# Moving a 128-point Hadamard transform from the FFN's activations onto its down weights, in a two-block transformer tower on one core

## Chip, cores, metric

The kernel is one program on one core of a Trainium2 chip. The metric is device time in microseconds (us). The engines are TensorE (PE in the profile; its weight loads are listed apart as PEld), VectorE (DVE), ScalarE (ACT), GpSimd (POOL) and SyncE (SP), which here issues all the transfers. Each engine runs its own instructions in program order and waits on semaphores for the others.

## The reference, cut to what matters

256 tokens of width 512 (64 sequences of 4 positions) pass a patch embedding, a first attention with quantised activations and ternary weights, a mixture of 16 experts with top-2 routing, a second attention, and an FFN with Hadamard transforms. Only the last is touched:

```python
n = SU_ug.shape[0]                       # 512
x = fwht(x * SU_ug) / SCALE
x_up = x @ W_up.T * (Wscale_ug[:INTER] * SCALE)
x_gate = x @ W_gate.T * (Wscale_ug[INTER:] * SCALE)
x = jax.nn.silu(x_gate) * x_up           # 256 tokens x 2048
x = fwht(x * SU_dp) / SCALE              # 2048-point transform
x = x @ W_down.T * (Wscale_dp * SCALE)   # 2048 -> 512
```

`fwht` is the normalised Walsh-Hadamard transform, a symmetric matrix of +1 and -1. The 2048 features lie as 16 chunks of 128: partitions hold the position in a chunk. The 2048-point transform is therefore a 128-point transform inside each chunk and a 16-point one across the chunks. Since both are linear, either can be applied to the activations or to the rows of the down weights.

## The kernel before, in words

Products are made in a split form: each fp32 operand is a high part (rounded by ACT to fp32r) plus a low part (the rest, taken by DVE), and three products high-high, high-low and low-high are added in PSUM. Names with `_hi` and `_lo` are these parts. A few products, the transposes (line 668) and the sums over prod (lines 787 and 939), are plain fp32.

The order on each engine is written out by hand. In the order of time:

- First attention (to about 64 us of the profiled span). At its end PE makes `transposes(2)`, issues 20 filler matmuls (`keep_warm`, line 701, products nobody reads), then `transposes(3)`; the router and the experts follow.
- Experts, `unit(n)` and `dn(p)`. Beside them DVE folds `down_raw` (the down weights, 16 chunks of 128x512) with the part of the 16-point transform that combines chunks c, c+4, c+8, c+12: `fold_piece(0)` to `fold_piece(3)` for the chunks 0, 1, 4, 5, 8, 9, 12, 13, then pieces 4 to 7 for the others. When all is done DVE sets `fold_done`.
- Second attention (from about 180 us). PE: `warm_up(2, ...)` with 24 fillers, `transposes(4)`, 5 fillers, the qkv products of token tile 0 and 1, then for each tile t fillers (3 and 8), `values(t)` and the output projection.
- FFN, `for f in range(FC)`. `ffn_gu(f)` on PE makes gate and up of chunk f, 24 matmuls of 256 columns. ACT takes the silu, DVE the product (`fglu`, line 1619, into `M["h"]`), ACT the high part of it (`fh_hi`, line 648), DVE the low part (`fh_ready`, line 1624), and PE the 128-point transform of chunk f, `rotate(f)`: two matmuls (lines 1000 and 1001) into bank 3 or 7. After four chunks ACT copies one bank to `M["a"]` (line 655) and DVE adds and subtracts (`within_pairs`, lines 1590 and 1591; `across_pairs`, line 1600), which is the rest of the 16-point transform. Then u is split (`u_high`, `u_low`) and multiplied by the split down weights (`wd_high`, `wd_low`, `down(c)`, 6 matmuls of 512 columns), which run some 7 chunks behind.
- SP issues the loads in one order. `l1_w` (second attention's weights, 2560 KB) stands before a wait for `side_done` 8, and `down_w` (4096 KB) behind the wait, since it overwrites the weights of the first attention. `f_low(f)` (line 1493) is the low part of the FFN weights of chunk f.

`tb(t, n)` is PSUM bank 4t + n. The functions that the change touches:

Of the kernel before, what the change touches and what calls it, by code (L numbers as in the profile page):

```python
# [75 lines left out]
def tower(nc, patches, tok_w, tok_b, att_w, router, moe_gu, moe_dn, l1_w, vec_cols, ws_dp, ffn_w,  # L76
          down_w, consts, out):
    with ExitStack() as ctx:
# [94 lines left out]
        fsilu, fglu, fh_hi, fh_ready = sem("fsilu"), sem("fglu"), sem("fh_hi"), sem("fh_ready")  # L173
        hd_done, hd_copied, hd_read = sem("hd_done"), sem("hd_copied"), sem("hd_read")
# [5 lines left out]
        XT_BANK = (1, 2, 1, 2, 1)  # L180

# [60 lines left out]
        with ExitStack() as s:  # L242
            M["silu"] = [sb(f"fs{j}", [P, TOK], F32, s) for j in range(2)]
            M["h"] = [sb(f"fh{j}", [P, TOK], F32, s) for j in range(2)]
            M["h_hi"] = [sb(f"fhh{j}", [P, TOK], F32R, s) for j in range(4)]
            M["h_lo"] = [sb(f"fhl{j}", [P, TOK], F32R, s) for j in range(4)]
            M["a"] = sb("fa", [P, 2, TOK], F32, s)
# [98 lines left out]
        def _(sp):  # L346
# [22 lines left out]
            sp.dma_start(l1_raw[:], l1_w).then_inc(ld_l1, 16)  # L369
            sp.wait_ge(side_done, 8)  # L370
            sp.dma_start(big_raw[:], down_w).then_inc(ld_down, 16)
            for p in range(2, PAIRS):
# [58 lines left out]
        def _(act):  # L431
# [100 lines left out]

            xt_high(2)
            xt_high(3)
            act.wait_ge(h_ready0, 2)
# [46 lines left out]

            xt_high(4)
            xt_high(5)
# [37 lines left out]
            def wd_high(c):  # L622
                if c == 0:
                    act.wait_ge(fold_done, 1)
                if c >= 4:
                    act.wait_ge(down_done, c - 3)
# [9 lines left out]
            for f in range(FC):  # L636
# [26 lines left out]
        def _(pe):  # L663
# [145 lines left out]

            transposes(2, B["xn"], 0)  # L810
            keep_warm(bank[3], GAP)
# [82 lines left out]
            for n in range(3):  # L894
                unit(n, False)
# [20 lines left out]
            warm_up(2, bank[3], WARM[1])  # L916
            transposes(4, L["xn"], 0)
            keep_warm(bank[3], 5)
            pe.wait_ge(w1_ready, KC)
            for t in range(TILES):  # L920
                for dst, a, b in ((tb(t, 3)[:, 0:QKV1 - C], C, QKV1), (tb(t, 2)[:], 0, C)):
                    pe.wait_ge(xt_hi_ready, 5 + t)
# [20 lines left out]
            for t in range(TILES):  # L943
                warm_up(3 + t, bank[1], 3 + 5 * t)
# [7 lines left out]

            transposes(8, M["xn"], 0)
# [40 lines left out]
            def rotate(f):  # L994

                pe.wait_ge(fh_ready, f + 1)
                if f >= 4 and f % 4 < 2:
                    pe.wait_ge(hd_read if f % 2 else hd_copied, f // 4)
                dst = tb(f % 2, 3)[:, f % 4 // 2 * TOK:(f % 4 // 2 + 1) * TOK]
# [713 lines left out]
```

## Time and profile before

| what | value |
|---|---|
| median of 3 runs | 301.54 us (300.75 to 302.03) |
| profiled execution, its own time | 300.32 us |
| its span, first to last instruction | 298.5 us |
| busy: PE / DVE / ACT | 275.4 (92%) / 236.9 (79%) / 146.8 us (49%) |
| mean granted TensorE clock | 0.973 |

The span is 1.8 us shorter than the time of the same execution. Busy shares are means over stages that are limited by different engines, so they tell little alone. PE's busy time includes the filler matmuls, which are 122 in number.

### The profile page before, as it was taken

How to read it: one execution, taken by the hardware profiler on the slowest of the kernel's cores; microseconds unless marked ns; L12 is line 12 of the kernel's file. 1: busy time of each engine (PE TensorE's matmuls, PEld its weight loads, DVE VectorE, ACT ScalarE, POOL GpSimd, SP SyncE). 2: the span in 40 equal slices, each digit the busy share in tenths (PEclk: the TensorE clock that was granted, in tenths of full speed). 3: DMA queues.
4: the chain of work that ended last, by engine and by line, in shares of the span. 5: the costliest groups of instructions: out<-in, count | busy, mean ns of one | idle time of the engine just before them, and what ended most of it. 6: DMA issues, size and time to landing. Idle time of an engine off the chain costs nothing. (4 is left out here: it accounts for less than half of the span.)

```text
span 298.5 us, 4692 instructions
## 1 busy us (share of the span) xinstructions
PE 275.4 (92%) x1807; PEld 238.3 (80%) x1807; DVE 236.9 (79%) x439; ACT 146.8 (49%) x238; POOL 10.0 (3%) x30
## 2 busy tenths in 40 slices
PE   8899399599989999999999999977999999999993
PEld 3555266499979899999999979857899999999862
DVE  1979997878496999899898877798628895778683
ACT  3989640024644665645655432322137773773640
POOL 0200000010000000000000004000000000000000
PEclk9999789977999999999999999999999999999998
DMA  6941599905034835546400049094000000000003
GB/s 255 414 186 36 187 378 418 419 4 189 26 137 183 307 117 211 193 157 242 151 0 3 0 143 419 2 356 209 0 0 2 0 3 0 2 1 2 0 0 70
DMA packets 6567, 40.47 MB, mean 136 GB/s; under 512 B 1169, under 2 KB 1425, under 8 KB 5266
## 3 DMA queue, kind: packets, MB, share of 16 engines
q1 hardware_dynamic: 6546, 40.18, 35.4%
q8 instruction: 14, 0.23, 0.3%
q14 instruction: 7, 0.06, 0.1%
HBM read 39.13 MB, written 0.52 MB: 133 GB/s over the span
## 5 line engine op out<-in xcount | busy, mean ns | idle before, releaser
L870 PE MATMUL bank<-s_xt_hi,s_gu_hi 128*128 128x256 f32 x120 | 34.0, 283 | 0.0
L871 PE MATMUL bank<-s_xt_lo,s_gu_hi 128*128 128x256 f32 x120 | 33.9, 283 | 0.0
L872 PE MATMUL bank<-s_xt_hi,s_gu_lo 128*128 128x256 f32 x120 | 33.9, 282 | 0.0
L984 PE MATMUL bank<-s_xf_hi,s_f_hi 128*128 128x256 f32 x128 | 31.3, 283 | 0.1
L984 PE MATMUL bank<-s_xf_hi,s_f_lo 128*128 128x256 f32 x128 | 31.1, 282 | 0.0
L459 ACT CAST s_xt_hi<-bank 128x512 fp32r<-128x512 f32 x10 | 5.9, 587 | 39.2 <-PE bank L668 33.3
L984 PEld LDWEIGHTS bank<-s_xf_hi,s_f_hi 128*128 128x128 f32 x128 | 24.1, 188 | 0.7 <-ACT s_xf_hi L619 0.4
L1493 DVE TENSOR_TENSOR s_f_lo<-s_ffn_raw,s_f_hi 128x1024 fp32r<-128x1024 f32 x16 | 19.6, 1225 | 6.1 <-ACT s_f_hi L592 6.1
L984 PEld LDWEIGHTS bank<-s_xf_hi,s_f_lo 128*128 128x128 f32 x128 | 24.1, 188 | 0.3
L871 PEld LDWEIGHTS bank<-s_xt_lo,s_gu_hi 128*128 128x128 f32 x120 | 23.0, 191 | 0.2
L870 PEld LDWEIGHTS bank<-s_xt_hi,s_gu_hi 128*128 128x128 f32 x120 | 23.0, 191 | 0.3
L872 PEld LDWEIGHTS bank<-s_xt_hi,s_gu_lo 128*128 128x128 f32 x120 | 23.0, 191 | 0.0
L466 ACT CAST s_gu_hi<-s_moe_raw 128x1024 fp32r<-128x1024 f32 x16 | 16.7, 1047 | 10.4 <-PE bank L872 10.3
L674 PE MATMUL bank<-s_dn_hi,s_ht_hi 128*128 128x512 f32 x48 | 19.3, 401 | 1.9 <-DVE s_ht_lo L1370 1.4
L526 ACT CAST s_ht_hi<-s_hm 128x256 fp32r<-128x256 f32 x24 | 9.6, 407 | 22.0 <-DVE s_hm L1364 22.0
L1288 DVE TENSOR_TENSOR s_gu_lo<-s_moe_raw,s_gu_hi 128x1024 fp32r<-128x1024 f32 x16 | 19.4, 1217 | 0.5 <-ACT s_gu_hi L466 0.5
L701 PE MATMUL bank<-s_had 128*128 128x256 f32 x122 | 18.9, 307 | 0.6 <-DVEq L1538 0.6
L639 ACT ACTIVATE s_fs<-bank,s_cols 128x256 f32<-128x256 f32 x16 | 7.6, 475 | 23.1 <-PE bank L990 23.1
L676 PE MATMUL bank<-s_dn_hi,s_ht_lo 128*128 128x512 f32 x48 | 18.8, 391 | 0.0
L675 PE MATMUL bank<-s_dn_lo,s_ht_hi 128*128 128x512 f32 x48 | 18.8, 391 | 0.0
L701 PEld LDWEIGHTS bank<-s_had 128*128 128x128 f32 x122 | 17.0, 207 | 1.6 <-DVEq L1538 1.0
L872 PE MATMUL bank<-s_xt_hi,s_rest_lo 128*128 128x256 f32 x64 | 18.1, 283 | 0.0
(249 smaller groups left out, 725.0 us busy)
## 6 DMA issues: line engine op xcount, KB each, us to landing
s_moe_raw<-moe_gu SPq DMA_DIRECT2D x16, 768.0 KB, 5.9
s_ffn_raw<-ffn_w SPq DMA_DIRECT2D x4, 2048.0 KB, 9.8
s_moe_raw<-moe_dn SPq DMA_DIRECT2D x8, 768.0 KB, 4.3
s_big_raw<-att_w SPq DMA_DIRECT2D x4, 1024.0 KB, 8.0
s_big_raw<-down_w SPq DMA_DIRECT2D x1, 4096.0 KB, 25.3
s_l_raw<-l_w SPq DMA_DIRECT2D x1, 2560.0 KB, 15.2
out<-s_h SPq DMA_DIRECT2D x4, 128.0 KB, 2.3
s_tok_w<-tok_w SPq DMA_DIRECT2D x1, 256.0 KB, 2.7
```

Of the source, the lines that this page charges most:

```text
L466: act.copy(B["gu_hi"][e % 2][:], main_of(e)).then_inc(guh_ready, 1)
L526: act.copy(B["ht_hi"][p % 2][:, part, :], B["hm"][n % 4][:]).then_inc(h_hi, 1)
L674: pe.matmul(dst, x_hi, w_hi, start=first, stop=False)
L675: pe.matmul(dst, x_hi, w_lo, start=False, stop=False)
L676: return pe.matmul(dst, x_lo, w_hi, start=False, stop=last)
L701: pe.matmul(spare_bank[:, 0:TOK].rearrange("p (i n) -> p i n", i=2), had[:], had[:].unsqueeze(1).to_broadcast([P, 2, P]), start=True, stop ...
L870: pe.matmul(dst, w_hi, xt_hi[:, k, :], start=(k == 0), stop=False)
L871: pe.matmul(dst, w_hi, xt_lo[:, k, :], start=False, stop=False)
L872: last = pe.matmul(dst, w_lo, xt_hi[:, k, :], start=False, stop=(k == KC - 1))
L984: pe.matmul(tb(j, n)[:, 0:TOK], M[w][j][:, k, n * P:(n + 1) * P], M["xf_hi"][:, k, :], start=(w == "w_hi" and k == 0), stop=False)
L1288: dve.tensor_tensor(B["gu_lo"][e % 2][:], main_of(e), B["gu_hi"][e % 2][:].bitcast(F32), ALU.subtract).then_inc(gu_ready, 1)
L1493: dve.tensor_tensor(M["w_lo"][f % 2][:], ffn_chunk_raw(f), M["w_hi"][f % 2][:].bitcast(F32), ALU.subtract).then_inc(fw_ready, 1)
```

## The change

The 128-point transform is applied to each chunk of `down_raw` instead of each chunk of h. `turn(i)` on PE makes one plain fp32 product of the Hadamard matrix (in `con`) with a chunk of 128x512 and `turned_back(i)` on ACT copies the bank back over the chunk. Eight chunks (those that `fold_piece(0)` to `(3)` combine) are turned before the fold, at the end of the first attention; the other eight after it, in the second attention. They stand where fillers stood. `down_w` is loaded ahead of `l1_w`. In the FFN `rotate`, the split of h and the copy to `M["a"]` are gone; `within_pairs` reads h itself from SBUF.

```diff
+        TURN_FIRST, TURN_LAST = (0, 1, 4, 5, 8, 9, 12, 13), (2, 3, 6, 7, 10, 11, 14, 15)
 (SP)
-            sp.dma_start(l1_raw[:], l1_w).then_inc(ld_l1, 16)
             sp.wait_ge(side_done, 8)
             sp.dma_start(big_raw[:], down_w).then_inc(ld_down, 16)
+            sp.dma_start(l1_raw[:], l1_w).then_inc(ld_l1, 16)
 (ACT)
+            def turned_back(i, ps):
+                c = (TURN_FIRST + TURN_LAST)[i]
+                act.wait_ge(turn_done, i + 1)
+                act.copy(down_raw[:, c, :], ps[:]).then_inc(turned, 1)
...
+            for i in range(3):
+                turned_back(i, bank[3 + 4 * (i % 2)])
             xt_high(2)
+            for i in range(3, 7):
+                turned_back(i, bank[3 + 4 * (i % 2)])
             xt_high(3)
+            turned_back(7, bank[7])
...
+            for i in range(8, 11):
+                turned_back(i, bank[3 + 4 * (i % 2)])
             xt_high(4)
+            turned_back(11, bank[7])
             xt_high(5)
...
             f_high(1)
+            turned_back(12, bank[1])
             xt_high(6)
             exp(3, L["sc"][:, 2, 1, 0:4], L["sc"][:, 3, 1, 0:4])
+            turned_back(13, bank[5])
             act.activation(spare1[:], neg_half[:], ACT.Silu)
+            turned_back(14, bank[1])
+            turned_back(15, bank[5])
             xt_high(7)
...
-                act.wait_ge(fglu, f + 1)
-                if f >= 4:
-                    act.wait_ge(hd_done, f - 3)
-                act.copy(M["h_hi"][f % 4][:], M["h"][j][:]).then_inc(fh_hi, 1)
                 for c in wd_of(f):
                     wd_high(c)
-                if f % 4 == 3:
-                    act.wait_ge(hd_done, f)
-                    if f >= 4:
-                        act.wait_ge(hd_read, f // 4)
-                    act.copy(M["a"][:], tb(0, 3)[:].rearrange("p (i n) -> p i n", i=2)).then_inc(hd_copied, 1)
 (PE)
+            def turn(i, ps, copied):
+                c = (TURN_FIRST + TURN_LAST)[i]
+                if i == 0:
+                    pe.wait_ge(ld_down, 16)
+                if i == len(TURN_FIRST):
+                    pe.wait_ge(fold_done, 1)
+                if copied:
+                    pe.wait_ge(turned, copied)
+                pe.matmul(ps[:], con[:, K_H:K_H + P], down_raw[:, c, :], start=True, stop=True).then_inc(turn_done, 1)
...
+            for i in range(3):
+                turn(i, bank[3 + 4 * (i % 2)], max(i - 1, 0))
             transposes(2, B["xn"], 0)
-            keep_warm(bank[3], GAP)
+            for i in range(3, 8):
+                turn(i, bank[3 + 4 * (i % 2)], i - 1)
             transposes(3, B["xn"], 1)
...
-            warm_up(2, bank[3], WARM[1])
+            for i in range(8, 11):
+                turn(i, bank[3 + 4 * (i % 2)], i - 1 if i > 9 else i)
             transposes(4, L["xn"], 0)
-            keep_warm(bank[3], 5)
+            turn(11, bank[7], 10)
             pe.wait_ge(w1_ready, KC)
+            pe.wait_ge(turned, 11)
...
-                warm_up(3 + t, bank[1], 3 + 5 * t)
+                if t == 0:
+                    turn(12, bank[1], 12)
+                else:
+                    turn(13, bank[5], 12)
+                    turn(14, bank[1], 13)
+                    turn(15, bank[5], 14)
                 values(t)
...
-            def rotate(f):
-                pe.wait_ge(fh_ready, f + 1)
...
-                pe.matmul(dst, had[:], M["h_hi"][f % 4][:], start=True, stop=False)
-                pe.matmul(dst, had[:], M["h_lo"][f % 4][:], start=False, stop=True).then_inc(hd_done, 1)
...
-                if f >= 1:
-                    rotate(f - 1)
 (DVE)
-                    dve.wait_ge(ld_down, 16)
+                    dve.wait_ge(turned, len(TURN_FIRST))
...
-                dve.wait_ge(hd_copied, g + 1)
-                dve.wait_ge(hd_done, 4 * g + 4)
-                odd = tb(1, 3)[:].rearrange("p (i n) -> p i n", i=2)
-                o.mark(dve.tensor_tensor(half_rotated[:, 0:2], M["a"][:], odd, ALU.add))
+                dve.wait_ge(fglu, 4 * g + 4)
+                even, odd = M["h"][g % 2][:, 0:4:2, :], M["h"][g % 2][:, 1:4:2, :]
+                o.mark(dve.tensor_tensor(half_rotated[:, 0:2], even, odd, ALU.add))
...
-                dve.wait_ge(fh_hi, f + 1)
-                dve.tensor_tensor(M["h_lo"][f % 4][:], M["h"][j][:], M["h_hi"][f % 4][:].bitcast(F32), ALU.subtract
-                                  ).then_inc(fh_ready, 1)
```

PE at the end of the first attention before, from its last projection products to the transposes of the second token tile (`s_con` holds both the identity and the Hadamard matrix, `s_had` is the filler's operand):

```order
L795 MATMUL bank4<-s_tern_p,s_xt_hi 128x512 x4
L687 MATMUL bank4<-s_tern_p,s_xt_lo 128x512 x4
L668 MATMUL bank2<-s_con,s_prod0 128x128 x4
L701 MATMUL bank3<-s_had 128x256 x20
L668 MATMUL bank6<-s_con,s_prod0 128x128 x4
```

The same place now; `s_big_raw` is the down weights:

```order
L695 MATMUL bank4<-s_tern_p,s_xt_lo 128x512 x4
L727 MATMUL bank3<-s_big_raw,s_con 128x512
L727 MATMUL bank7<-s_big_raw,s_con 128x512
L727 MATMUL bank3<-s_big_raw,s_con 128x512
L676 MATMUL bank2<-s_con,s_prod0 128x128 x4
L727 MATMUL bank7<-s_big_raw,s_con 128x512
L727 MATMUL bank3<-s_big_raw,s_con 128x512
L727 MATMUL bank7<-s_big_raw,s_con 128x512
L727 MATMUL bank3<-s_big_raw,s_con 128x512
L727 MATMUL bank7<-s_big_raw,s_con 128x512
L676 MATMUL bank6<-s_con,s_prod0 128x128 x4
```

Three fp32 products stand ahead of the first transposes, where nothing stood, and five take the place of the 20 fillers.

PE at the start of the second attention before, from the last expert product to the first qkv products:

```order
L676 MATMUL bank4<-s_dn_hi,s_ht_lo1 128x512
L701 MATMUL bank3<-s_had 128x256 x24
L668 MATMUL bank1<-s_con,s_xn2 128x128 x4
L701 MATMUL bank3<-s_had 128x256 x5
L681 MATMUL bank3<-s_w1_hi,s_xt_hi 128x256
```

The same place now:

```order
L684 MATMUL bank4<-s_dn_hi,s_ht_lo1 128x512
L727 MATMUL bank3<-s_big_raw,s_con 128x512
L727 MATMUL bank7<-s_big_raw,s_con 128x512
L727 MATMUL bank3<-s_big_raw,s_con 128x512
L676 MATMUL bank1<-s_con,s_xn2 128x128 x4
L727 MATMUL bank7<-s_big_raw,s_con 128x512
L689 MATMUL bank3<-s_w1_hi,s_xt_hi 128x256
```

Three products replace 24 fillers ahead of the transposes, and one replaces 5 behind them.

DVE at the end of the FFN before, from the product of the last chunk on (`s_fh` is h, `s_fhl` its low part, `s_fa` is `M["a"]`):

```order
L1619 SCALAR_TENSOR_TENSOR s_fh1<-bank5,s_cols,s_fs1 128x256
L1624 TENSOR_TENSOR s_fhl3<-s_fh1,s_fhh3 128x256
L1611 TENSOR_TENSOR s_wd_lo<-s_big_raw,s_wd_hi 128x512
L1590 TENSOR_TENSOR s_half_rotated<-s_fa,bank7 128x512
L1591 TENSOR_TENSOR s_half_rotated<-s_fa,bank7 128x512
```

The same place now:

```order
L1642 SCALAR_TENSOR_TENSOR s_fh1<-bank5,s_cols,s_fs1 128x256
L1632 TENSOR_TENSOR s_wd_lo<-s_big_raw,s_wd_hi 128x512
L1611 TENSOR_TENSOR s_half_rotated<-s_fh1 128x512
L1612 TENSOR_TENSOR s_half_rotated<-s_fh1 128x512
L1632 TENSOR_TENSOR s_wd_lo<-s_big_raw,s_wd_hi 128x512
```

The low part of h is gone, and the additions of pairs follow the product with one other operation between.

## Rows read from the trace of the kernel before

**Rows 1.** Windows: PE, PEld, DVE, ACT, POOL busy, clock, DMA share, GB/s

```profile
65.00:179.70 114.70, 112.75 (x792) 105.67 (x792) 99.89 (x173) 61.03 (x111) 0.00 (x0) 0.99 0.37 136
179.70:219.40 39.70, 35.68 (x240) 31.81 (x239) 28.52 (x56) 9.87 (x17) 5.17 (x12) 1.00 0.44 179
219.40:287.00 67.60, 67.27 (x490) 63.00 (x488) 52.56 (x84) 41.30 (x73) 0.00 (x0) 1.00 0.01 1
```

**Rows 2.** Timeline around the end of the FFN: start, us, engine, line [idle before]

```profile
280.67 0.28 PE L1000 MATMUL bank<-s_fhh,s_had 128*128 128x256 f32 x1
280.79 0.28 PE L1001 MATMUL bank<-s_fhl,s_had 128*128 128x256 f32 x1
...
280.94 0.48 DVE L1619 SCALAR_TENSOR_TENSOR s_fh<-bank,s_cols,s_fs 128x256 f32<-128x256 f32 x1 [0.94 <-ACT s_fs L639]
...
282.42 0.69 DVE L1611 TENSOR_TENSOR s_wd_lo<-s_big_raw,s_wd_hi 128x512 fp32r<-128x512 f32 x1
...
283.03 0.68 DVE L1590 TENSOR_TENSOR s_half_rotated<-s_fa,bank 128x512 f32<-128x512 f32 x1
...
287.46 0.47 PE L674 MATMUL bank<-s_wd_hi,s_u_hi 128*128 128x512 f32 x1 [0.36 <-DVE s_u_lo L1606]
```

**Rows 3.** Instructions of line 787: duration in ns, first and last start

```profile
L787 PE MATMUL bank<-s_prod,s_con x16: 590/593/593, 42.2 to 48.6; 128*128 128x512 f32 x16
```

**Rows 4.** Windows of PE alone: busy, clock, DMA share, GB/s

```profile
42.20:49.00 6.80, 6.80 (x18) 1.00 0.98 368
...
61.00:64.00 3.00, 2.66 (x13) 0.50 0.00 0
...
68.00:70.50 2.50, 2.50 (x13) 0.50 0.00 0
```

**Rows 5.** Timeline of SP's issues before the experts' loads

```profile
35.81 0.48 SPq L369 DMA_DIRECT2D s_l_raw<-l_w  x1
36.33 0.44 SPq L371 DMA_DIRECT2D s_big_raw<-down_w  x1
```

**Rows 6.** The page's DMA issues: count, KB each, median us to landing

```profile
s_big_raw<-down_w SPq DMA_DIRECT2D x1, 4096.0 KB, 25.3
s_l_raw<-l_w SPq DMA_DIRECT2D x1, 2560.0 KB, 15.2
```

**Rows 7.** Timeline of PE at the end of the first attention

```profile
55.21 1.07 PE L687 MATMUL bank<-s_tern_p,s_xt_lo 128*128 128x512 f32 x4
59.40 0.66 PE L668 MATMUL bank<-s_con,s_prod 128*128 128x128 f32 x4 [3.12 <-DVE s_prod L1048]
59.81 3.85 PE L701 MATMUL bank<-s_had 128*128 128x256 f32 x20
64.09 0.68 PE L668 MATMUL bank<-s_con,s_prod 128*128 128x128 f32 x4 [0.43 <-DVE s_prod L1048]
```

**Rows 8.** Timeline at the start of the second attention

```profile
179.72 3.04 PE L701 MATMUL bank<-s_had 128*128 128x256 f32 x24
...
182.59 0.60 PE L668 MATMUL bank<-s_con,s_xn 128*128 128x128 f32 x4
...
183.23 0.59 ACT L459 CAST s_xt_hi<-bank 128x512 fp32r<-128x512 f32 x1 [4.02 <-PE bank L668]
...
183.96 0.36 PE L681 MATMUL bank<-s_w_hi,s_xt_hi 128*128 128x256 f32 x1 [0.17 <-ACT s_xt_hi L459]
...
189.65 0.69 DVE L1517 TENSOR_TENSOR s_prod<-s_kv,s_q 128x512 f32<-128x512 f32 x1 [0.90 <-ACT s_q L600]
```

**Rows 9.** Timeline of PE around the two value sums

```profile
194.84 2.02 PE L939 MATMUL bank<-s_con,s_prod 128*128 128x128 f32 x16 [0.54 <-DVE s_prod L1551]
...
199.81 0.86 PE L687 MATMUL bank<-s_o_hi,s_xt_lo 128*128 128x512 f32 x3
...
203.37 3.81 PE L939 MATMUL bank<-s_con,s_prod 128*128 128x128 f32 x32 [0.93 <-DVE s_prod L1551]
```

**Rows 10.** The page's costly groups: line, count, busy us, mean ns, idle before

```profile
L1493 DVE TENSOR_TENSOR s_f_lo<-s_ffn_raw,s_f_hi 128x1024 fp32r<-128x1024 f32 x16 | 19.6, 1225 | 6.1 <-ACT s_f_hi L592 6.1
```

More of the change, by code:

```diff
@@ L172, in tower @@
         fwh_ready, fw_ready, fg_done, fu_done = sem("fwh_ready"), sem("fw_ready"), sem("fg_done"), sem("fu_done")
-        fsilu, fglu, fh_hi, fh_ready = sem("fsilu"), sem("fglu"), sem("fh_hi"), sem("fh_ready")
-        hd_done, hd_copied, hd_read = sem("hd_done"), sem("hd_copied"), sem("hd_read")
+        fsilu, fglu = sem("fsilu"), sem("fglu")
+        turn_done, turned, hd_read = sem("turn_done"), sem("turned"), sem("hd_read")
         u_raw, u_hi, u_ready, wdh_ready, wd_ready, down_done = sem("u_raw"), sem("u_hi"), sem("u_ready"), sem("wdh_ready"), sem("wd_ready"), sem("down_done")
@@ L243, in tower @@
             M["silu"] = [sb(f"fs{j}", [P, TOK], F32, s) for j in range(2)]
[L244 to L247, printed above, removed]
+            M["h"] = [sb(f"fh{j}", [P, 4, TOK], F32, s) for j in range(2)]
             M["u"] = sb("u", [P, 4, TOK], F32, s)
@@ L624, in wd_high @@
                     act.wait_ge(fold_done, 1)
+                    act.wait_ge(turned, FC)
                 if c >= 4:
@@ L894, in _ @@
             for n in range(3):
+                if n == 2:
+                    pe.wait_ge(turned, 8)
                 unit(n, False)
@@ L913, in _ @@
             dn(PAIRS - 1)
-            warm_up(2, bank[3], WARM[1])
+            for i in range(8, 11):
+                turn(i, bank[3 + 4 * (i % 2)], i - 1 if i > 9 else i)
             transposes(4, L["xn"], 0)
-            keep_warm(bank[3], 5)
+            turn(11, bank[7], 10)
             pe.wait_ge(w1_ready, KC)
+            pe.wait_ge(turned, 11)
             for t in range(TILES):
                 for dst, a, b in ((tb(t, 3)[:, 0:QKV1 - C], C, QKV1), (tb(t, 2)[:], 0, C)):
+                    if t == 1:
+                        pe.wait_ge(turned, 12)
                     pe.wait_ge(xt_hi_ready, 5 + t)
@@ L950, in _ @@
                 low_products(tb(t, 3)[:], t, lambda k: L["o_hi"][:, k, :]).then_inc(proj_done, 1)
+            pe.wait_ge(turned, FC)
             transposes(8, M["xn"], 0)
@@ L992, in ffn_gu @@
                     last.then_inc(done, 1)
-            def rotate(f):
-                pe.wait_ge(fh_ready, f + 1)
-                if f >= 4 and f % 4 < 2:
-                    pe.wait_ge(hd_read if f % 2 else hd_copied, f // 4)
-                dst = tb(f % 2, 3)[:, f % 4 // 2 * TOK:(f % 4 // 2 + 1) * TOK]
-                pe.matmul(dst, had[:], M["h_hi"][f % 4][:], start=True, stop=False)
-                pe.matmul(dst, had[:], M["h_lo"][f % 4][:], start=False, stop=True).then_inc(hd_done, 1)
             def down_tile(c, t):
@@ L1016, in _ @@
                 ffn_gu(f)
-                if f >= 1:
-                    rotate(f - 1)
                 if f >= 7:
                     down(f - 7)
-            rotate(FC - 1)
             for c in range(9, FC - 4):
@@ L1585, in within_pairs @@
             def within_pairs(g):
-                dve.wait_ge(hd_copied, g + 1)
-                dve.wait_ge(hd_done, 4 * g + 4)
-                odd = tb(1, 3)[:].rearrange("p (i n) -> p i n", i=2)
-                o.mark(dve.tensor_tensor(half_rotated[:, 0:2], M["a"][:], odd, ALU.add))
-                dve.tensor_tensor(half_rotated[:, 2:4], M["a"][:], odd, ALU.subtract).then_inc(hd_read, 1)
+                dve.wait_ge(fglu, 4 * g + 4)
+                even, odd = M["h"][g % 2][:, 0:4:2, :], M["h"][g % 2][:, 1:4:2, :]
+                o.mark(dve.tensor_tensor(half_rotated[:, 0:2], even, odd, ALU.add))
+                dve.tensor_tensor(half_rotated[:, 2:4], even, odd, ALU.subtract).then_inc(hd_read, 1)
             def across_pairs(g):
@@ L1618, in _ @@
                 dve.wait_ge(fu_done, f + 1)
-                dve.scalar_tensor_tensor(M["h"][j][:], tb(j, 1)[:, 0:TOK], wsu_c[:, f:f + 1], M["silu"][j][:],
+                if f >= 8:
+                    dve.wait_ge(hd_read, f // 4 - 1)
+                dve.scalar_tensor_tensor(M["h"][f // 4 % 2][:, f % 4, :], tb(j, 1)[:, 0:TOK], wsu_c[:, f:f + 1], M["silu"][j][:],
                                          ALU.mult, ALU.mult).then_inc(fglu, 1)
```

## The prediction, as put on record before the kernel ran

> **What bounds the kernel now.** I read the windows by stage first, to see which engine is full where. PE is busy 112.75 of 114.70 us in the experts and 67.27 of 67.60 us in the FFN, while DVE has 99.89 and 52.56 us of work there and ACT 61.03 and 41.30; in the second attention PE has 35.68 of 39.70 us, and part of that is fillers [rows 1]. So real PE work that leaves the FFN shortens it one for one, and PE time added in place of fillers costs only what overhangs them. Then the timelines of the places that the change touches, to see who waits for whom. At the end of the first attention PE sits idle 3.12 us and then runs 20 fillers; both transposes wait for DVE's xn (the releaser in both rows) [rows 7]. At the start of the second attention the chain is xn, transposes, ACT's copy, qkv products, and DVE waits 0.90 us for q at 189.65 [rows 8]: what delays PE there delays all that follows. At the very end PE waits 0.36 us for DVE's u_low [rows 2]: the last stretch hangs on DVE's chain from the last h.
>
> **What leaves the FFN.** `rotate` is two matmuls per chunk, issued 0.12 us apart (280.67, 280.79) although each lasts 0.28, since they overlap [rows 2]. A chunk costs PE 2 x 0.12 = 0.24 us. Fifteen rotates stand ahead of the last chunk's gate and up: 15 x 0.24 = 3.6 us, all on the full engine. From then on the end is set by DVE. Before, 2.09 us pass from the last h (280.94) to the first addition of pairs (283.03), filled by ACT's high part, DVE's low part, the last rotate, ACT's copy and one wd_low [rows 2]. Now only h (0.48) and wd_low stand there. Lengths include an overlap with the next instruction, so I take 0.48 + 0.69 = 1.17, plus 0.1 for ACT's cast of wd, which wd_low waits for: 1.26. Gain 0.83. Behind the first addition DVE's queue is the same as before, back to back up to u_low. PE arrives there 16 x 0.24 = 3.84 earlier for its matmuls and some 0.4 earlier for the last rotate that held it, against 4.43 for DVE, so its wait of 0.36 stays about as it is. **FFN: -(3.6 + 0.83) = -4.4 us.** The additions read h from SBUF instead of one operand from a bank; I take the same 0.68 us. ACT's 16 casts and 4 copies and DVE's 16 low parts are worth nothing by themselves, PE being the full engine.
>
> **What a turn costs.** The trace has no such product, but line 787 has the same shape in fp32 with moving data of 512 columns. Its loop issues 8 products and the trace shows 16 instructions, so one is two. Their starts run from 42.2 to 48.6: 6.4/15 = 0.43 us apart, 0.86 per product, the last ending 0.59 after its start [rows 3], at a granted clock of 1.00 [rows 4]. ACT's copy of a bank is 0.59 us [rows 8]. A release takes 0.04 us from PE to ACT (182.59 + 0.60 = 183.19 to 183.23) and 0.14 from ACT to PE (183.82 to 183.96) [rows 8].
>
> **First attention.** Before, PE's last product ends at 56.28 and the next could be issued at some 56.12. Three turns end their issue at 56.12 + 3 x 0.86 = 58.70, under the idle time to 59.40 with 0.7 us to spare [rows 7]. The weights must be there: before, `down_w` lands at 36.33 + 25.3 = 61.6 and `l1_w` at 35.81 + 15.2 = 51.0 [rows 5, 6]. The two land one behind the other, 10.6 us for 4096 KB, so 2560 KB take 6.6 us and `down_w` ahead of them lands at 55.0, 1.1 us before PE asks. `l1_w` then lands near 61.6, where `down_w` did, and is first read by ACT in the experts. Five turns follow the transposes at 59.81. Two banks alternate, so two turns take at least product 1.02, release 0.04, copy 0.59, release 0.14 = 1.79, 0.90 a turn; with the first at 0.86 they end at 64.10 to 64.25 against 64.09 for the transposes [rows 7]. ACT's copy for the router stands behind turned copy 6, which is done by then. **+0.15 us**, and PE's fullness in the experts [rows 1] passes it on. The DVE fold waits for 8 turned chunks only some 30 us later, at no cost.
>
> **Second attention, start.** Turn 8 begins at 179.72 where the 24 fillers did and ends at 180.74. Turn 9 waits for its copy: 180.78 + 0.59 + 0.14 = 181.51. Turn 10 follows at 182.37 and the transposes at 183.22, against 182.59. ACT takes copy 9 before, then copy 10 from 183.42 to 184.01, and only then the copy of xt, which waits in ACT's queue behind it: to 184.60, PE at 184.74 against 183.96 [rows 8]. Turn 11 (183.62 to 184.48) is under that. The whole stage follows q: **+0.75 us**.
>
> **Second attention, values.** Turn 12 takes the place of 3 fillers and 0.54 us of idle before 194.84 and fits. Turns 13 to 15 can be issued when the projection's products are out, at 199.81 + 3 x 0.23 = 200.51, without the fillers' wait for DVE. They need 3 x 0.86 to 203.1, or 203.2 since turn 15 waits for copy 13, which stands behind ACT's exp; the value sum began at 203.37 after 0.93 us of idle [rows 9]. From there PE runs 3.81 us by itself, so an overhang would cost in full. I take **+0.05 us**. Their copies finish well before ACT's next xt.
>
> **Sum.** -4.4 + 0.15 + 0.75 + 0.05 = -3.5 us. The profiled execution took 300.32 us, which gives 296.8. It lies 1.2 us under the median of the runs, 301.54, from which I count: **298.0 us**. A measurement of this kernel can tell about 0.5%, 1.5 us, from no change.
>
> **The rivals.**
>
> *The clock falls under the turns.* Before, the clock was 0.50 at 61 to 64, after the idle at 56 to 59, and 0.50 at 68 to 70.5, after the router's products of 16 columns [rows 4, 7]. A turn at the lower level (1.2 instead of 2.4 GHz) takes 1.71 us. If turns 3 to 7 run there, 5 x 0.86 = +4.3, which gives 302.3. Against it: three turns now lie in that idle time, and fp32 products back to back kept 1.00 for 6.8 us [rows 4]. Chance 0.08. The Trainium skill (TensorE: Matmul & The Clock Gate, "A second HAM failure mode: psum-queue depth-cycling") says that a stream which cycles through PSUM banks, with small waits between its groups, can make the clock swing, which is the pattern of turn, copy, turn. The trace so far speaks against it; by the page this rival would be the forecast.
>
> *The weights come late (slower).* If `down_w` does not land ahead of `l1_w` but with it, near 61.6, turn 0 starts 5.5 us late, less 0.7 to spare: +4.8, so 302.8; an idle time of that length lowers the clock as the shorter one did, and turns 0 to 7 at 1.71 add up to 6.9: 302.8 to 309.7, say 305. It decides from a landing at 56.1 + 0.7 + 3.5 = 60.3 on. Against it stand the two landings 10.6 us apart. Chance 0.05. The Trainium skill (DMA: Bandwidth & Descriptors, "Queues, rings and completion order") has descriptors of one ring consumed in order but no first-in-first-out completion for an issuing engine; here the share of the DMA engines was 0.98 while the two loads ran [rows 4], each load being spread over all of them, so I keep it small.
>
> *DVE or ACT becomes the FFN's bound.* Without `rotate` a chunk is 24 x 0.12 = 2.88 us of PE. In chunks 4 to 6 DVE has h 0.48, f_low 1.23 [rows 2, 10] and two operations of 0.68: 3.1 at most. If the first six rotates are not given back, 6 x 0.24 = 1.4 us is lost: 299.4. For it speaks that DVE's margin is thin there; against it that before the ratio was the same (DVE 0.4 more, PE 0.24 more) and PE had no gap. Chance 0.10.
>
> *More than that.* The denser stream could keep the clock up through 68 to 70.5 too; the 3 us at half rate would give 1.5 back: 296.5. The router's small products stay as they are. Chance 0.08.
>
> **The numbers.** The forecast, 297 to 299.3, has 0.69. With the rivals at 302.3, 305, 299.4 and 296.5 the range 295.8 to 300.6 leaves out the first two and a little on each side, under 0.2; its upper end takes in an overhang of some 1 us in each attention beside a smaller gain at the end. Faster by over 0.5% (under 300.0): 0.69 + 0.10 + 0.08 less some at the edges = 0.84. Within: 0.10, of which most is the clock's rival. Slower: 0.06.
>
> **What would show it.** The turn's group: 32 instructions of 0.59, 0.43 apart; `down_w` landing at 55 with PE's idle time before turn 0 gone; transposes at 64.2, qkv products 0.9 later than before, the value sums not later than that; in the FFN a chunk shorter by 0.24 with PE at 99%; from the last h to the first addition some 1.25 us. It is wrong if turns are spaced by more than 0.9, if the clock under them shows 0.50, or if PE in the FFN gets idle before DVE.

## The result, and the profile after

| | before | changed |
|---|---|---|
| median of 6 interleaved runs | 301.86 us | 298.31 us |
| lowest to highest | 300.75 to 303.58 | 294.98 to 298.71 |
| profiled execution | 300.32 us | 297.94 us |
| its span, mean granted clock | 298.5 us, 0.973 | 296.1 us, 0.979 |

The changed kernel takes 0.987 of the time before (95% interval 0.9831 to 0.9909): 3.55 us less by the medians, where 3.5 was forecast. A second set of runs of it gave 297.59 us, 0.9864 (0.9823 to 0.9905).

The two profiled spans differ by 2.4 us only, because the one after starts late: the last group of PE's products in the first attention (four, shown as one row) begins at 56.57 us, against 55.21 before [rows 7]. This event is the reference event in all that follows. The delay is there before anything that was changed: the first transfer of the swapped keys goes out at 28.45 us, against 26.92 before, since ACT waited 0.5 us longer for the first attention weights and 1.0 us longer for DVE. A second profiled execution of the changed kernel has that transfer at 27.25. So a good part of the delay is chance; that all of it is, is not shown, for the reference event lies at 55.2 to 56.0 in the three profiles with the old order of loads and at 55.9 to 57.6 in the nine with the new one. Everything below is therefore measured from an event that both kernels have, not from the start of the span.

**The weights.** The timeline of SP's issues after, and the page's DMA issues (count, KB each, us to landing):

```profile
37.84 0.33 SPq L368 DMA_DIRECT2D s_big_raw<-down_w  x1
38.22 0.45 SPq L369 DMA_DIRECT2D s_l_raw<-l_w  x1
```
```profile
s_big_raw<-down_w SPq DMA_DIRECT2D x1, 4096.0 KB, 20.0
s_l_raw<-l_w SPq DMA_DIRECT2D x1, 2560.0 KB, 25.6
```

`down_w` lands at 37.84 + 20.0 = 57.84 and the other at 63.8, one behind the other again, as before [rows 5, 6]. With the late start added, the forecast of 55.0 becomes 56.4: it is 1.4 us late, and all of the 1.1 us to spare is used up. The 20.0 us are this execution's; in the eight other profiles with this order the load took 18.3 or 18.4 us. The later landing of `l1_w` (63.8 instead of 51.0) cost nothing, as the length of the experts below shows.

**The turns.** All instructions of the turned products: duration in ns (least, median, most), first and last start, shapes:

```profile
L727 PE MATMUL bank<-s_big_raw,s_con x32: 590/592/697, 57.9 to 205.0; 128*128 128x512 f32 x32
```

The timeline of PE at the end of the first attention of the changed kernel (start, us, engine, line, operation, count, [idle before <-releaser]):

```profile
56.57 1.07 PE L695 MATMUL bank<-s_tern_p,s_xt_lo 128*128 128x512 f32 x4
57.89 2.93 PE L727 MATMUL bank<-s_big_raw,s_con 128*128 128x512 f32 x6 [0.24 <-DMA s_big_raw<-down_w]
60.76 0.66 PE L676 MATMUL bank<-s_con,s_prod 128*128 128x128 f32 x4
61.25 4.63 PE L727 MATMUL bank<-s_big_raw,s_con 128*128 128x512 f32 x10
65.72 0.60 PE L676 MATMUL bank<-s_con,s_prod 128*128 128x128 f32 x4
```

Turn 0 waits 0.24 us for the weights. Three turns (6 instructions) still fit under what was 3.12 us of idle time: the transposes come 60.76 - 56.57 = 4.19 us after the reference event, and before it was 59.40 - 55.21 = 4.19 [rows 7]. The five turns behind them take 4.47 us to the second transposes; in all 9.15 us pass, against 8.88 before, so this place costs +0.27, where +0.15 was forecast. Windows of the same kernel (PE, PEld, DVE, ACT, POOL busy, clock, DMA share, GB/s) show the clock under the turns at full:

```profile
52.00:68.00 16.00, 15.66 (x72) 9.68 (x70) 12.93 (x29) 6.94 (x12) 1.61 (x4) 1.00 0.55 235
69.00:72.00 3.00, 3.00 (x16) 3.00 (x16) 2.67 (x8) 0.35 (x2) 0.00 (x0) 0.50 0.00 0
```

The stretch at half clock behind the router is there as it was before [rows 4]. From the second transposes to PE's first instruction behind the last expert product it is 115.57 us, and was 115.63.

**Second attention, start**, PE and ACT in the timeline of the changed kernel:

```profile
181.29 1.02 PE L727 MATMUL bank<-s_big_raw,s_con 128*128 128x512 f32 x2
182.35 0.59 ACT L464 COPY s_big_raw<-bank 128x512 f32<-128x512 f32 x1 [1.55 <-PE bank L727]
182.99 1.98 PE L727 MATMUL bank<-s_big_raw,s_con 128*128 128x512 f32 x4 [0.68 <-ACT s_big_raw L464]
184.81 0.60 PE L676 MATMUL bank<-s_con,s_xn 128*128 128x128 f32 x4
185.01 0.59 ACT L464 COPY s_big_raw<-bank 128x512 f32<-128x512 f32 x1 [0.27 <-PE bank L727]
185.49 0.59 ACT L457 CAST s_xt_hi<-bank 128x512 fp32r<-128x512 f32 x1
186.23 0.36 PE L689 MATMUL bank<-s_w_hi,s_xt_hi 128*128 128x256 f32 x1
```

It went as worked out: turn 9 waits 0.68 us for copy 8, and ACT takes copy 10 ahead of the cast of xt. The first product of the projection comes 186.23 - 181.29 = 4.94 us after the first turn, against 183.96 - 179.72 = 4.24 after the first filler [rows 8]: +0.70, forecast +0.75.

**Values**, PE in the timeline of the changed kernel:

```profile
201.82 1.09 PE L695 MATMUL bank<-s_o_hi,s_xt_lo 128*128 128x512 f32 x4
202.75 2.82 PE L727 MATMUL bank<-s_big_raw,s_con 128*128 128x512 f32 x6
205.62 3.81 PE L967 MATMUL bank<-s_con,s_prod 128*128 128x128 f32 x32
```

The last value sum starts 2.25 us later than before [rows 9], and the first projection product of this attention came 186.23 - 183.96 = 2.27 later. Turns 12 to 15 cost nothing.

**FFN.** Stages of the changed kernel as windows (columns as above), and the timeline of DVE at its end:

```profile
67.00:181.30 114.30, 112.35 (x788) 105.23 (x789) 99.88 (x173) 61.18 (x111) 0.00 (x0) 0.99 0.38 137
181.30:221.60 40.30, 37.70 (x216) 29.43 (x214) 28.43 (x56) 14.05 (x25) 5.17 (x12) 1.00 0.43 175
221.60:284.00 62.40, 61.95 (x455) 58.58 (x455) 46.77 (x67) 33.67 (x52) 0.00 (x0) 1.00 0.00 1
```
```profile
279.56 0.48 DVE L1642 SCALAR_TENSOR_TENSOR s_fh<-bank,s_cols,s_fs 128x256 f32<-128x256 f32 x1 [1.84 <-ACT s_fs L656]
280.05 0.69 DVE L1632 TENSOR_TENSOR s_wd_lo<-s_big_raw,s_wd_hi 128x512 fp32r<-128x512 f32 x1
280.66 0.69 DVE L1611 TENSOR_TENSOR s_half_rotated<-s_fh 128x512 f32<-128x512 f32 x1
```
```profile
286.22 0.51 PE L682 MATMUL bank<-s_wd_hi,s_u_hi 128*128 128x512 f32 x1 [0.18 <-DVE s_wd_lo L1632]
```

PE stays full (61.95 of 62.40 us), and the gap between it and the others has grown: DVE has 46.77. Counted from PE's first product of the transform that opens the stage (215.53 before, 217.79 after), the last h comes 3.64 us earlier than before (forecast 3.6). From the last h to the first addition of pairs it is 280.66 - 279.56 = 1.10 us where it was 2.09 [rows 2] (forecast 1.26). With both, the FFN is 4.61 us shorter to DVE's last addition, that of the residual (78.99 before, 74.38 after).

The sum of the profiled spans: +1.36 before any changed instruction, +0.27, -0.06 in the experts, +0.70, 0 and -4.61 make -2.34, and 298.5 - 296.1 is 2.4. Without the late start it is -3.7, beside -3.55 by the medians of the runs.

### The profile page after: what moved, and what is told of

Read it like the earlier page. It is cut to its first block and busy times, and to the rows that moved or that the text cites. A ratio compares the mean times of both kernels' runs of the same rounds, so it can differ in the third digit from the quotient of the medians.

```text
span 296.1 us, 4530 instructions
## 1 busy us (share of the span) xinstructions
PE 276.2 (93%) x1744; PEld 231.0 (78%) x1747; DVE 231.7 (78%) x423; ACT 148.7 (50%) x234; POOL 10.0 (3%) x30
## 5 line engine op out<-in xcount | busy, mean ns | idle before, releaser
L893 PE MATMUL bank<-s_xt_lo,s_rest_hi 128*128 128x256 f32 x64 | 18.1, 283 | 0.0
L892 PE MATMUL bank<-s_xt_hi,s_rest_hi 128*128 128x256 f32 x64 | 18.1, 283 | 0.0
L1024 PE MATMUL bank<-s_xf_lo,s_f_hi 128*128 128x256 f32 x128 | 17.8, 281 | 0.0
```

The costliest lines, as they stand in the source:

```text
L892: pe.matmul(dst, w_hi, xt_hi[:, k, :], start=(k == 0), stop=False)
L893: pe.matmul(dst, w_hi, xt_lo[:, k, :], start=False, stop=False)
L1024: last = pe.matmul(tb(j, n)[:, 0:TOK], M["w_hi"][j][:, k, n * P:(n + 1) * P], M["xf_lo"][:, k, :], start=False, stop=(k == KC - 1))
```

## The experiments

The kernel before ran beside each; a ratio is to it. Theory: the gain is all in the FFN (PE's rotates and the shorter chain), the turns are almost free since they stand in place of idle time and fillers, and they are free only because `down_w` lands first. The rivals: the turns change the clock; the FFN is bound by DVE, so that its casts and low parts are what paid.

**One half alone.** `e1_ffn_only` is the kernel before with the edits to the FFN's h and `rotate` only, so the 128-point transform is left out. `e2_turns_only` has the turns and the order of loads and keeps `rotate`.

```
 e1 (to before):
-                act.copy(M["h_hi"][f % 4][:], M["h"][j][:]).then_inc(fh_hi, 1)
...
-                if f >= 1:
-                    rotate(f - 1)
 e2 (to before):
-            sp.dma_start(l1_raw[:], l1_w).then_inc(ld_l1, 16)
             sp.wait_ge(side_done, 8)
             sp.dma_start(big_raw[:], down_w).then_inc(ld_down, 16)
+            sp.dma_start(l1_raw[:], l1_w).then_inc(ld_l1, 16)
...
+            for i in range(8, 11):
+                turn(i, bank[3 + 4 * (i % 2)], i - 1 if i > 9 else i)
```

> The kernel before with only the FFN half of the change: rotate, the split of h and the copy to M["a"] are gone, and nothing is turned (the 128-point transform is left out altogether, so this part of the computation is missing; fillers, loads and both attentions are those of before). My theory: the whole gain sits here and the turns cost 0.9 us (0.2 in the first attention, 0.7 in the second). Then this kernel is 4.6 us under before, about 297.2 (ratio 0.985), and 0.9 under the changed kernel. Rival: the denser PE stream of the turns gives back clock, and the FFN alone is worth less than the whole, 3.5 us or under, ratio 0.988 or more. Rival: DVE bounds the FFN, 3.2 us or under.

> The kernel before with only the other half: all 16 turns, their copies and the load order of the changed kernel, while rotate stays in the FFN (the 128-point transform is applied twice). My theory: 0.9 us over before (0.2 and 0.7), about 302.7, ratio 1.003, below what a measurement can tell from nothing. Rival of the clock's gift: no cost or a gain of up to 1 us, ratio 0.997. Rival of a hidden cost elsewhere (the late load of the second attention's weights, ACT's fuller queue): 2 us or more over before, ratio 1.007 or more.

Measured: e1 296.71 us, 0.9849 (0.9822 to 0.9877); e2 302.1 us, 1.0013 (0.9987 to 1.0039). The two parts add up to the change, -1.5% and +0.1%, and the larger one is the FFN's. The cost of the turns is within the noise of the runs; it is read from the traces. e1 holds a surprise, seen in its timeline of PE and its windows:

```profile
60.16 0.66 PE L658 MATMUL bank<-s_con,s_prod 128*128 128x128 f32 x4 [3.11 <-DVE s_prod L1026]
60.57 2.63 PE L691 MATMUL bank<-s_had 128*128 128x256 f32 x20
64.85 0.65 PE L658 MATMUL bank<-s_con,s_prod 128*128 128x128 f32 x4 [1.66 <-DVE s_prod L1026]
```
```profile
60.00:63.00 3.00, 2.84 (x24) 2.83 (x24) 2.80 (x7) 0.59 (x1) 0.00 (x0) 1.00 0.03 11
```

The idle time of 3.11 us is there as before, but the clock stayed at 1.00 and the 20 fillers took 2.63 us, not 3.85 [rows 7]. The second transposes came no earlier for it (8.87 us after the reference event, 8.88 before): DVE sets their time. So an idle time of that length does not always lower the clock, and here its level costs nothing.

e2's profiled execution had no half-clock stretch behind the router. The first two of the expert products that stand there, in the trace of the kernel before and then of e2:

```profile
66.76 1.39 PE L853 MATMUL bank<-s_xt_hi,s_gu_hi 128*128 128x256 f32 x8
68.65 2.05 PE L853 MATMUL bank<-s_xt_lo,s_gu_hi 128*128 128x256 f32 x8
```
```profile
67.59 1.20 PE L888 MATMUL bank<-s_xt_hi,s_gu_hi 128*128 128x256 f32 x8
69.00 1.20 PE L888 MATMUL bank<-s_xt_lo,s_gu_hi 128*128 128x256 f32 x8
```

From the second transposes to the end of the expert products e2 took 114.00 us instead of 115.63: the half-clock stretch is worth 1.6 us. Four of e2's twelve runs had a mean clock of 0.990 or 0.991 and took 299.7 to 300.2 us; the others, at 0.977 to 0.983, took 301.4 to 302.9. The two groups are some 2.4 us apart, more than this stretch is worth, so more than it differs between them.

**The order of loads.** `e4_old_load_order` is the changed kernel with the layer's weights issued first again.

```
+            sp.dma_start(l1_raw[:], l1_w).then_inc(ld_l1, 16)
             sp.wait_ge(side_done, 8)
             sp.dma_start(big_raw[:], down_w).then_inc(ld_down, 16)
-            sp.dma_start(l1_raw[:], l1_w).then_inc(ld_l1, 16)
```

> The changed kernel with the old order of loads: l1_w ahead of down_w. My theory: down_w then lands some 6 us later, near 63, turn 0 waits for it and PE idles 5 us; the transposes behind it are late by 4.8 us, and since that idle time lowers the clock, some turns run at the lower level: 303 to 306 us, slower than before (ratio 1.005 to 1.015). Rival: the loads share the engines and land together whatever the order, so it costs under 1 us and the time stays near 298.

Measured: 303.41 us, 1.0081 (1.0054 to 1.0109). By the ratios this is 2.1% or 6.4 us above the changed kernel. The timeline of PE and a window:

```profile
55.46 1.07 PE L695 MATMUL bank<-s_tern_p,s_xt_lo 128*128 128x512 f32 x4
61.84 5.49 PE L727 MATMUL bank<-s_big_raw,s_con 128*128 128x512 f32 x6 [5.31 <-DMA s_big_raw<-down_w]
67.12 0.95 PE L676 MATMUL bank<-s_con,s_prod 128*128 128x128 f32 x4
67.91 4.62 PE L727 MATMUL bank<-s_big_raw,s_con 128*128 128x512 f32 x10
72.37 0.60 PE L676 MATMUL bank<-s_con,s_prod 128*128 128x128 f32 x4
```
```profile
62.00:67.00 5.00, 5.00 (x6) 1.89 (x7) 0.78 (x3) 1.17 (x2) 1.06 (x3) 0.50 0.00 0
```

The wait for `down_w` is 5.31 us, then the clock is 0.50 (its lower level, 1.2 GHz) and three turns take 5.49 us instead of 2.82; the next five run at full clock. The second transposes come 16.91 us after the reference event instead of 9.15: +7.8 us in this place, of which this execution got some 1.5 back, having no half-clock stretch behind the router: 6.3, as the ratios have it. This is the slower rival of the prediction, made real: the two lines on SP's queue are what keeps the change from being a loss.

**The wait of turn 9.** `e3_two_deep` lets turn 9 start without copy 8, whose bank it does not use.

```
-                turn(i, bank[3 + 4 * (i % 2)], i - 1 if i > 9 else i)
+                turn(i, bank[3 + 4 * (i % 2)], i - 1)
```

> The changed kernel with one number changed: turn 9 no longer waits for the copy of turn 8, so two products are under way at the start of the second attention as everywhere else. My theory: the 0.7 us of that place come from this wait (PE idle 0.68 us between turn 8 and 9); without it the first qkv product starts 4.2 to 4.4 us after the last expert product instead of 4.9, and the time falls by 0.6 us to 297.7, ratio 0.985. Rival: ACT's queue sets that place (copy 10 stands ahead of the copy of xt), and less than 0.2 us comes back.

Measured: 296.77 us, 0.9848 (0.9813 to 0.9882). PE in its timeline:

```profile
181.39 2.82 PE L727 MATMUL bank<-s_big_raw,s_con 128*128 128x512 f32 x6
184.10 0.66 PE L676 MATMUL bank<-s_con,s_xn 128*128 128x128 f32 x4
...
186.55 0.60 PE L676 MATMUL bank<-s_con,s_xn 128*128 128x128 f32 x4
```

The three turns run back to back and the transposes follow 2.71 us after the first turn, where they stood 2.87 us after the first filler before [rows 8]. The next transposes, which stand behind the first products, come at 5.16 us; 5.27 before and 5.96 in the changed kernel. So the whole 0.7 at this place was that one wait, and it comes back. That is read from the traces; the intervals of e3 and the changed kernel overlap. PE's row of the first three turns of e3, and the row of its weight loads for the third of them, show one thing more:

```profile
57.67 2.82 PE L727 MATMUL bank<-s_big_raw,s_con 128*128 128x512 f32 x6
59.36 0.30 PEld L727 LDWEIGHTS bank<-s_big_raw,s_con 128*128 128x128 f32 x2 [0.65 <-ACT s_big_raw L464]
```

The third turn writes the bank of the first, so its weight load waits for ACT's copy of that bank. Six instructions of 0.59, all 0.43 apart, would take 2.74 us; they take 2.82, the 0.08 more being spent in the turn that waited.

**What in the FFN paid.** `e5_pe_load_back` adds two filler products of 256 columns per chunk, the PE work of `rotate` with no data behind it. `e6_split_back` adds the high and low part of h on ACT and DVE, which nothing reads, and no work of PE.

```
 e5:
+                if f >= 1:
+                    keep_warm(tb((f - 1) % 2, 3), 2)
 e6:
+                act.wait_ge(fglu, f + 1)
+                act.copy(M["h_hi"][f % 2][:], M["h"][f // 4 % 2][:, f % 4, :]).then_inc(fh_hi, 1)
...
+                dve.wait_ge(fh_hi, f + 1)
+                dve.tensor_tensor(M["h_lo"][f % 2][:], M["h"][f // 4 % 2][:, f % 4, :],
+                                  M["h_hi"][f % 2][:].bitcast(F32), ALU.subtract)
```

> The changed kernel with two filler matmuls of 256 columns per chunk (15 pairs) at the place where rotate stood in the FFN: PE's load is back, the split of h and its chain are not. My theory: PE is the full engine there, so 15 x 0.24 = 3.6 us come back one for one; the first addition of pairs still follows the last h after 1.1 us: 301.9 beside a before of 301.5, ratio 0.997 to 1.000. Rival: the gain of the FFN came from the shorter chain h, high part, low part, rotate that throttled PE, and the matmuls were cheap: then only 1 to 2 us come back, ratio 0.990 to 0.993.

> The changed kernel with ACT's high part and DVE's low part of each h back (results that nobody reads), without rotate: ACT's and DVE's load and waits are back, PE's is not. My theory: nothing comes back in the FFN's loop, where PE is full, and at its end the last h is followed by cast and low part again, about 0.8 us more before the first addition of pairs: +0.8 us, ratio 0.990. Rival (DVE or ACT bounds the FFN without rotate): the 16 casts and low parts, 0.8 us a chunk, are felt in the loop as well: +2 us or more, PE idle between chunks, ratio 0.994 or more.

Measured: e5 300.27 us, 0.9953 (0.9925 to 0.9982), between its two expectations; e6 299.58 us, 0.9931 (0.9901 to 0.996), nearer to the rival's. By the traces, e5 lost 2.9 us in the FFN, all ahead of the last h, and its chain behind the last h is 1.10 as in the changed kernel. Only 14 of the 15 pairs stand ahead of the last chunk's gate and up, 14 x 0.24 = 3.36 us, and PE's one wait of 0.30 us in the loop of the changed kernel is gone in e5; so nearly all of the added work is paid, and PE is the bound there. e6 lost 1.89 us: 0.98 in the chain behind the last h (2.08, as before the change), and 0.9 ahead of it, nearly all at one place, in e6's timeline of PE:

```profile
246.48 0.47 PE L686 MATMUL bank<-s_wd_hi,s_u_hi 128*128 128x512 f32 x1 [0.96 <-DVE s_u_lo L1631]
```

With rotates gone and DVE's low parts kept, DVE is late with the first low part of u, and PE stands for 0.96 us. The changed kernel has a trace of the same wait, 0.30 us. The low parts of DVE were priced at nothing in the prediction; without them gone, 0.9 of the 3.6 us would not have been had.

**Better than both.** DVE sits idle for 1.84 us ahead of the last h and has splits of down weights queued behind it, among them those of numbers 10 and 11. `e7_tail_order` is e3 with the splits of down weights 9 to 11 in chunk 14, none in chunk 15, and none of number 11 behind the loop.

```
 wd_of(f):
+            if f >= FC - 2:
+                return (FC - 7, FC - 6, FC - 5) if f == FC - 2 else ()
 ACT, DVE, behind the loop:
-            wd_high(FC - 5)
-            wd_low(FC - 5)
```

> The third experiment's kernel (turn 9 without its wait), and in addition the splits of down weights 10 and 11 on ACT and DVE are made before the last h, where DVE sits idle 1.8 us, instead of behind it. My theory: the end of the kernel hangs on DVE's chain from the last h; with two operations of 0.6 us less in it PE's waits of 0.2 us before the 13th and 0.6 us before the 14th down product vanish: 0.7 us less than the third experiment, ratio 0.982 to 0.983. Rival: ACT's wait for the buffer of weight 11 (for down product 7) delays the last silu, and nothing or a loss comes of it, ratio 0.985 or more.

Measured: 296.06 us, 0.9814 (0.9776 to 0.9852), the lowest median of all; 0.7 us less than e3 by the medians, though the intervals overlap. By the traces, from the last h to the last addition it is 0.7 us shorter than in e3. DVE in its timeline:

```profile
278.78 0.48 DVE L1643 SCALAR_TENSOR_TENSOR s_fh<-bank,s_cols,s_fs 128x256 f32<-128x256 f32 x1 [0.64 <-ACT s_fs L658]
279.30 0.69 DVE L1612 TENSOR_TENSOR s_half_rotated<-s_fh 128x512 f32<-128x512 f32 x1
```

The idle time falls from 1.84 to 0.64 us and the first addition follows the last h at 0.52 instead of 1.10. From there to its last product PE shows no wait any more, so this way offers nothing further.

**The half-clock stretch behind the router.** `e8_router_fillers` is e7 with three filler products on either side of the first low product of the router. `e9_two_more_products` is the changed kernel with two fp32 products of 512 columns ahead of the second transposes, work of known length on that path.

```
 e8:
+            keep_warm(bank[0], 3)
             router_low(0)
+            keep_warm(bank[0], 3)
 e9:
+            pe.matmul(bank[0][:], con[:, K_H:K_H + P], h[:, 0, :], start=True, stop=True)
+            pe.matmul(bank[0][:], con[:, K_H:K_H + P], h[:, 0, :], start=True, stop=True)
```

> The kernel of e7 with 3 fillers before and 3 behind the first tile's low router products, 0.7 us of PE work on a full engine. Theory of the clock: the low granted clock at 69 to 72 us follows the router's products of 16 columns; with fillers among them the clock stays at its upper level there, which gives back 1.5 us for 0.7 spent: 0.8 us less than e7, clock above 0.985. Rival: the level there hangs on something else (the phase of the run), and 0.7 us is simply added, ratio 0.985.

> The changed kernel with two more plain fp32 products of 512 columns (of no use, into bank 0) ahead of the transposes of the second token tile in the first attention, behind turn 7. My theory: the five turns there already overhang the work they replaced, so PE time added at this place is paid in full through the experts: +1.7 us against the changed kernel, ratio about 0.992 to 0.993. Rival: slack behind it (DVE's wait for the router, PE's idle time in the experts) takes it up, and less than 0.5 us shows; then the overhang of 0.2 us which I count for the turns was no cost either.

> The changed kernel itself once more, beside e9 on the same chip, as the reference for it. Theory and rivals alike: the ratio of the first measurement, 0.987, within its interval.

Measured: e8 296.15 us, 0.9832 (0.9794 to 0.9869), no better than e7. In its profiled execution the stretch is there all the same:

```profile
69.50:73.00 3.50, 3.50 (x20) 3.50 (x20) 2.84 (x7) 0.20 (x1) 0.00 (x0) 0.56 0.00 0
```

and the fillers are simply added, +0.70 from the second transposes to the end of the expert products. But four of its six runs had a mean clock of 0.988 (294.9 to 296.5 us), against two of e7's six at 0.988 or more, so whether the fillers make the stretch rarer is open.

e9 took 298.76 us, 0.9894 (0.9855 to 0.9933), and the changed kernel beside it (`e10_changed_again`) 297.59: 1.2 us more by the medians, with intervals that overlap, so the time alone decides nothing. Its timeline of PE and a window:

```profile
57.57 1.09 PE L695 MATMUL bank<-s_tern_p,s_xt_lo 128*128 128x512 f32 x4
...
66.70 1.02 PE L834 MATMUL bank<-s_h,s_con 128*128 128x512 f32 x2
67.56 1.02 PE L835 MATMUL bank<-s_h,s_con 128*128 128x512 f32 x2
68.41 0.60 PE L676 MATMUL bank<-s_con,s_prod 128*128 128x128 f32 x4
```
```profile
70.00:73.00 3.00, 3.00 (x28) 3.00 (x28) 3.00 (x5) 1.07 (x2) 0.00 (x0) 1.00 0.00 0
```

The second transposes come 10.84 us after the reference event instead of 9.11 to 9.15. All 1.7 us of the added work is passed on, so PE is the bound there once the turns are in. The two added products wait for nothing and are 67.56 - 66.70 = 0.86 us apart, with 0.85 to the transposes. Then the half-clock stretch was absent from this execution and gave 1.5 us back: 114.03 us to the end of the expert products, as in e2 (114.00), so nothing behind takes up the 1.7.

## Why the prediction was right

- **FFN -4.4: measured -4.61.** Ahead of the last h 3.6 was forecast and 3.64 measured, and the near match is luck. The prediction counts 15 rotates ahead of the last chunk's gate and up, but there are 14: `rotate(14)`, at 280.67 [rows 2], stands behind it. The work of 14 is 14 x 0.24 = 3.36 us. The other 0.3 came from a term that the prediction put at nothing (next point). Behind the last h 0.83 was forecast and 0.99 measured: the 0.1 set aside for ACT's cast of wd was not needed, and h and the first addition stand 1.10 apart with one operation between, where 1.17 was taken. The FFN's part is shown by e1 (the gain without the turns) and e5 (2.9 of it gone when PE's work is put back).
- **ACT's and DVE's work on h "worth nothing by themselves, PE being the full engine": wrong in part.** Before, PE stood in `rotate` for the low part of h at two places, where the two products start 0.22 apart instead of 0.12 and the first of them comes late too (timeline of PE before; the third row is the last chunk's gate and up, which ends ahead of the rotate at 280.67):

```profile
225.62 0.39 PE L1000 MATMUL bank<-s_fhh,s_had 128*128 128x256 f32 x1
225.84 0.28 PE L1001 MATMUL bank<-s_fhl,s_had 128*128 128x256 f32 x1
...
279.73 1.11 PE L990 MATMUL bank<-s_xf_lo,s_f_hi 128*128 128x256 f32 x8
```

  The two places, at 225.6 and 244.4, cost some 0.3 us together, and that made up for the miscounted rotate. e5 agrees: with PE's work of before but no split of h, its last h comes 0.7 us earlier in the stage than before. e6 shows 0.9 us ahead of the last h for the split alone, nearly all at one place. The forecast did not suffer, since both works leave together. The third rival, DVE as the bound, was thus near: it is what one would have with `rotate` gone and the low parts kept.
- **A turn: 32 instructions of 0.59, 0.43 apart, 0.86 us: right where it waits for nothing.** e9's two added products show it (0.86 and 0.85). Where a turn waits for the copy of its bank it takes 0.08 more, in the first attention every second one, and two turns take 1.80 us, which is the 1.79 that the prediction worked out from product, copy and releases. At the lower clock a turn takes 1.7 us in e4 (three in 67.12 - 61.84 = 5.28, a wait's 0.16 included), as forecast.
- **First attention +0.15: measured +0.27** in the changed kernel, 0.23 to 0.27 in the other executions that have these turns, this order of loads and nothing added there. The +0.15 was the upper end of 64.10 to 64.25 and has the copies' pace in it already. What it lacked is mostly the start of turn 3: 61.25 - 60.76 = 0.49 us behind the transposes, where the first filler stood 59.81 - 59.40 = 0.41 behind them [rows 7].
- **`down_w` at 55.0: right in kind, and late by chance in this execution.** It landed at 57.84, 20.0 us after its issue. In the eight other profiles with this order it took 18.3 or 18.4 us from issue to landing (in the second profile of the changed kernel it landed at 55.04), and it was there 1.2 to 2.2 us before PE asked, where 1.1 was forecast. Here the margin was all used up, to a wait of 0.24. Behind it stands the second margin, the 0.7 us by which three turns are shorter than the idle time, and that took it up.
- **Second attention +0.75: measured +0.70**, by the very waits named; e3 takes them away.
- **Values +0.05: measured 0** (-0.02 by the two starts).
- **The clock's rival did not come**: 1.00 under all turns. The Trainium skill (TensorE: Matmul & The Clock Gate, "A second HAM failure mode: psum-queue depth-cycling") tells of a kernel whose clock swings with such small waits, and would have made it the forecast. The traces here do not agree: five turns alternating between two banks, each bank waiting for its copy, ran at 1.00 in the changed kernel, in e2, e3 and e9. In e4 three turns ran at 0.50, but behind 5.31 us without a product, and the five behind them at 1.00.
- **The late weights' rival: mechanism right, price near its lower end.** The forecast for that landing was 302.8 to 309.7, with eight turns at the lower clock; e4, with that landing, took 303.41, and only three turns ran there.
- **The third rival's 1.4 us:** PE waits once in the FFN's loop, 0.30 us.
- **The faster rival's 1.5 us** is the right price for the half-clock stretch (1.5 to 1.6 measured), but both profiled executions of the changed kernel have the stretch, with a denser stream ahead of it than before.

Before the first experiment the sum was no proof: errors can cancel, and two did, the fifteenth rotate and the low parts priced at nothing. The cost of the places, 0.27 and 0.70, and the gain of 4.61 are each in the trace where the sum had them, and e1 to e6 each move one part. The mechanism (PE work leaves the full stage one for one, and lands where fillers and idle time were) is shown; the match of 3.55 us with 3.5 is closer than some of its terms, which are up to 0.2 us off.

## What to carry to other kernels

A transform that sits on the activations in a full stretch can go onto the weights if an earlier stretch has idle time or fillers on that engine; price it by where it leaves and where it lands, and then ask when its operand lands in memory, for here the order of two loads was worth 6 us and the sign of the result. Two products on two banks with a copy each need no wait for the copy of the other bank: such a wait, written once too strictly, cost 0.7 us. When an engine idles ahead of the last operand of a chain, look in its queue behind that operand for work that can stand ahead of it.

## What was not expected of the hardware

- The half-clock stretch of 3 us behind the router's products of 16 columns was there in both profiles of the changed kernel and in most others, and absent in those of e2, e4 and e9. The runs' mean clocks suggest that it comes and goes within one kernel too, which no pair of profiles shows. The changed kernel's fastest run, 294.98 us, had a mean clock of 0.993; its eleven others in both sets, at 0.974 to 0.985, took 296.6 to 298.7 us. The change's gain is not the clock's: both profiles, before and after, have the stretch, and at one mean clock, 0.979, the changed kernel took 297.2 to 298.7 us and the kernel before 300.1 to 302.0. But the turns may make the stretch rarer: 23 of the 72 runs of the kernels with turns and `down_w` loaded first have a mean clock of 0.985 or more, and none of the 57 recorded ones of the kernel before is above 0.980. Since that kernel has another stretch at half clock, at 61 to 64 us [rows 4], its mean is lower in any case, and the count proves nothing by itself. What decides the stretch stays open; more work ahead of it (e9) and fillers in it (e8) did not settle it.
- The same 3.1 us without a product, at the same place, was followed by half clock in the kernel before and by full clock in e1.
